# Four waits moved, and h and the layer weights as float16 halves, in a two-layer graph network kernel on one core

## The reference

```
h = relu(layernorm(x))
x = x + relu([h, segment_sum(h[src], dst), segment_sum(edge_attr, dst)] @ L0_W.T + L0_b)
h = relu(layernorm(x))
h1 = relu(segment_mean(h[src], dst) @ W1_l + b1 + h @ W1_r)
h2 = relu(segment_mean(h1[src], dst) @ W2_l + b2 + h1 @ W2_r)
x = x + h2
```

## Time and profile before

| what | value |
|---|---|
| median of 3 runs | 1438.12 us (1434.83 to 1440.58) |
| the profiled execution, its own time | 1440.59 us |
| its span, first to last instruction | 1438.8 us |
| mean granted TensorE clock | 0.984 |
| TensorE (PE) busy | 1356.1 us, 94% |
| VectorE (DVE) busy | 808.3 us, 56% |
| GpSimd (POOL) busy | 653.0 us, 45% |
| ScalarE (ACT) busy | 492.2 us, 34% |

### The profile page before, as it was taken

How to read it: one execution, slowest core, us unless ns; L and a number is a source line. 1 busy time by engine, 2 the same in 40 slices (tenths; PEclk the granted TensorE clock), 3 DMA queues, 4 the chain that set the end, 5 groups by cost and what they waited for, 6 DMA issues and landing times.

```text
span 1438.8 us, 34983 instructions
## 1 busy us (share of the span) xinstructions
PE 1356.1 (94%) x12154; PEld 1229.2 (85%) x12155; DVE 808.3 (56%) x1830; ACT 492.2 (34%) x1398; POOL 653.0 (45%) x771
## 2 busy tenths in 40 slices
PE   3768999999999999999999999999999999999995
PEld 3657999999999998998888888788888888888884
DVE  8678999898888888883444545422222223222221
ACT  2731123456788888882232232211111110000000
POOL 5400001111112212116777666377777645777775
PEclk9978999999999999999999999999999999999997
DMA  6109678888899898886564565565656666666662
GB/s 183 29 2 250 201 221 244 240 247 258 262 269 273 264 274 263 255 261 204 200 216 156 166 234 141 181 204 191 208 186 203 169 203 193 220 209 217 212 214 62
DMA packets 284723, 294.49 MB, mean 205 GB/s; under 512 B 19461, under 2 KB 250064, under 8 KB 284672
## 3 DMA queue, kind: packets, MB, share of 16 engines
q1 hardware_dynamic: 233861, 212.90, 46.9%
q0 software_dynamic: 26016, 69.24, 17.1%
q10 hardware_dynamic: 24795, 11.74, 2.8%
HBM read 245.70 MB, written 48.11 MB: 204 GB/s over the span
## 4 chain that ended last, share of the span: by engine, by line
PE 70%; POOL 15%; issue 7%; DMA 3%; ACT 3%; DVE 3%; SPq 0%; ACTq 0%; POOLq 0%; DVEq 0%
PE edge_banks L1126 27%; PE edge_banks L1064 20%; POOL shared L862 15%; PE banks L1038 10%; PE edge_banks L1060 4%; PE edge_banks L1103 3%; PE banks L1144 3%; DMA x_sb<-in_x 1%; PE banks L926 1%; ACT own L1274 1%; DMA shared<-g_rows,list_src 1%; ACT shared L1331 1%; PE edge_banks L1133 1%; DVE edge_t L1482 1%; PE banks L1138 1%
## 5 line engine op out<-in xcount | busy, mean ns | idle before, releaser
L862 POOL DMA_INDIRECT shared<-g_rows,list_src x555 | 540.1, 973 | 232.3 <-issue 168.7
L1126 PE MATMUL edge_banks<-g_even,shared 128*128 128x257 f16 (+1 forms) x3822 | 443.3, 272 | 1.2 <-DVE shared L1690 1.2
L1126 PEld LDWEIGHTS edge_banks<-g_even,shared 128*128 128x128 fp8e3 x3822 | 371.5, 97 | 58.9 <-DVEq L1659 1.4
L1064 PE MATMUL edge_banks<-shared 128*128 128x128 f32 x2744 | 344.5, 276 | 7.0 <-issue 6.6
L1064 PEld LDWEIGHTS edge_banks<-shared 128*128 128x128 f32 x2744 | 324.8, 192 | 10.5 <-issue 10.4
L841 POOL DMA_DIRECT2D counts<-shared x156 | 76.4, 490 | 484.5 <-ACT shared L1331 469.3
L1716 DVE SCALAR_TENSOR_TENSOR shared<-edge_banks,shared,own 128x128 f32<-128x128 f32 x98 | 34.4, 351 | 367.9 <-PE edge_banks L1126 339.2
L1126 PE MATMUL edge_banks<-shared 128*128 128x256 f16 x1911 | 225.7, 272 | 0.2 <-DVE own L1698 0.2
L1627 DVE TENSOR_TENSOR shared<-iota,shared 128x3528 f16<-128x3528 f16 x98 | 195.5, 1995 | 39.6 <-PE banks L1038 39.2
L1331 ACT ACTIVATE shared<-banks 128x392 uint16<-128x392 f32 x312 | 152.1, 488 | 179.2 <-PE banks L1038 169.3
L1126 PEld LDWEIGHTS edge_banks<-shared 128*128 128x128 fp8e3 x1911 | 185.2, 97 | 30.7 <-DVE own L1698 0.5
(11 more groups left out here) (282 smaller groups left out, 982.1 us busy)
## 6 DMA issues: line engine op xcount, KB each, us to landing
shared<-in_edge_attr SPq DMA_DIRECT2D x195, 512.0 KB, 4.5
shared<-counts SPq DMA_DIRECT2D x117, 784.0 KB
counts<-shared POOLq DMA_DIRECT2D x156, 196.0 KB, 4.0
shared<-g_rows,list_src POOLq DMA_INDIRECT x555
shared<-hot_rows SPq DMA_DIRECT2D x20, 304.0 KB
g_rows<-g_even SPq DMA_DIRECT2D x1, 3136.0 KB, 15.7
g_rows<-shared ACTq DMA_DIRECT2D x49, 64.0 KB
g_rows<-g_even ACTq DMA_DIRECT2D x49, 64.0 KB
```

The source lines that it names most:

```text
L862: pool.indirect_dma_start(ring_g[use % RING][:, t, 0:2 * D], None, g_rows[r], bass.IndirectOffsetOnAxis(ap=list_src[:, at:at + 1], axis=0) ...
L1064: mm = pe.matmul(edge_wide[bank][:, :, at], ring[:, bank * GROUP_TILES + j, :], hot_dst[u][:, k, (j - 1) * SPREAD:j * SPREAD].unsqueeze(1) ...
L1126: mm = pe.matmul(acc[s][:, 0:wide], stream8[slot][:, order[h], :], G[r % 2][:, order[h], 0:wide], start=h == 0, stop=h == BLOCKS - 1, skip ...
```

## The change

1. *First one-hots.* VectorE's wait for `zeroed` at the start of the build becomes a wait for `list_turned` (signalled after the last transposes of the lists, before the zeros); the wait for `zeroed` stands before the first `hot_dst` now.
2. *Places of the lists.* In rounds 0 and 1 the first eight lists stand at 5, 10, ..., 40. Round 2 is unchanged. The list of the last target block has 15 tiles in place of 18, in all rounds.
3. *Last list in two parts.* The last 5 gathers of round 2's last list signal a semaphore of their own, and TensorE waits for it only before the last 5 tiles.
4. *End behind the branch.* SyncE, ScalarE and VectorE load the verdict once it is there and take the branch before their last work (the last block on VectorE, its store on ScalarE, the wait for the stores on SyncE).
5. *Halves.* In rounds 0 and 1, h is written as two float16 halves. In round 0 three VectorE instructions do it in place of the one on ScalarE; in round 1 two in place of one. The turn is two float16 matmuls of 128 columns with an identity; ScalarE's copy then moves 256 columns, to float16. The layer weights are split into halves and scaled once (`split_weights`, ahead of round 0's first block on VectorE), and the dense product is three float16 matmuls of 256 columns. The own term's instruction (L1698) becomes one with a scale.

```diff
-LIST_AT = (tuple(range(6, LOOP_TO, TURN_OF)) + (44, 47),) * 2 + (tuple(range(6, LOOP_TO, TURN_OF)) + (45, 48),)
+LIST_AT = (tuple(range(5, LOOP_TO[0], TURN_OF)) + (44, 47),) * 2 + (tuple(range(6, LOOP_TO[2], TURN_OF)) + (45, 48),)
+LAST_BLOCK_TILES, LATE_TILES = 15, 5
...
+        def tiles_of(k):
+            return LAST_BLOCK_TILES if DENSE + list_of(k) == BLOCKS - 1 else LIST_TILES[k % 2]
+        def late_tiles(r, k):
+            return LATE_TILES if r == ROUNDS - 1 and k == LISTED - 1 else 0
...
-                                                    ).then_inc(list_landed[use % RING], 16)
+                                                    ).then_inc(late_landed if late else list_landed[use % RING], 16)
...
                         for t in range(tiles):
+                            if late_tiles(r, k) and t == tiles - late_tiles(r, k):
+                                pe.wait_ge(late_landed, 16 * late_tiles(r, k))
...
-                            pe.transpose(turn_ps[o], h_blk[:, o, :], ident[:, :]).then_inc(R["turned"], 1)
+                            for k in range(2):
+                                mm = pe.matmul(turn_ps[o][:, k * D:(k + 1) * D], h16[:, o, k * D:(k + 1) * D], turn16, start=True, stop=True)
+                            mm.then_inc(R["turned"], 1)
...
-                            pe.matmul(g_ps[o], hT_blk[:, o, :], w_conv[:, 2 * to - 2:2 * to, :].rearrange("p k f -> p (k f)"),
-                                      start=True, stop=True).then_inc(R["g_up"], 1)
+                            high, low = hT16[:, o, 0:D], hT16[:, o, D:2 * D]
+                            pe.matmul(g_ps[o], high, w_high[:, to - 1, :], start=True, stop=False, skip_group_check=True)
+                            pe.matmul(g_ps[o], low, w_high[:, to - 1, :], start=False, stop=False, skip_group_check=True)
+                            pe.matmul(g_ps[o], high, w_low[:, to - 1, :], start=False, stop=True, skip_group_check=True).then_inc(R["g_up"], 1)
...
                     if r == 0:
                         pe.wait_ge(S["zeroed"], 2 * BANKS + 2 * NDUO)
+                        pe.wait_ge(S["w_edge_ready"], 2)
...
-                            act.activation(hT_blk[:, o, :], turn_ps[o], ACT.Copy).then_inc(R["hT_done"], 1)
+                            act.activation(hT16[:, o, :], turn_ps[o], ACT.Copy).then_inc(R["hT_done"], 1)
...
-                            act.activation(h_blk[:, s, :], x_sb[:, bs, :].rearrange("p a f -> p (a f)"), ACT.Relu,
-                                           bias=tiny[:, s, 2:3], scale=tiny[:, s, 1:2]).then_inc(R["h_done"], 1)
...
-                dve.wait_ge(S["zeroed"], 2 * BANKS)
+                dve.wait_ge(S["list_turned"], 1)
...
                         if first and u == 0:
+                            dve.wait_ge(S["zeroed"], 2 * BANKS)
                             dve.wait_ge(S["edge_cleared"], 3)
...
+                    link(dve.tensor_scalar(h_raw, a_x, tiny[:, s, 1:2], tiny[:, s, 2:3], ALU.mult, ALU.add))
+                    dve.wait_ge(R["turned"], n + 1)
+                    link(dve.tensor_scalar(h16[:, s, 0:D], h_raw, 0.0, None, ALU.max))
+                    dve.scalar_tensor_tensor(out=h16[:, s, D:2 * D], in0=h_raw, scalar=0.0, in1=h16[:, s, 0:D], op0=ALU.max, op1=ALU.subtract
+                                             ).then_inc(R["h_done"], 1)
...
+            held = sp.snap(verdict[0], donate=True, min_val=0, max_val=1)
             with sp.If(held < 1):
...
+            with sp.Else():
+                finish()
```

264 lines of the change are left out of this document (161 added, 103 removed).

## The result

| | kernel before | changed kernel |
|---|---|---|
| median of the runs | 1438.12 us (1434.83 to 1441.71, 5 runs) | 1428.82 us (1426.64 to 1431.87, 5 runs) |
| profiled execution, its span | 1440.59, 1438.8 us | 1431.87, 1430.1 us |

The ratio of the two is 0.9935, with a 95% interval of 0.9911 to 0.9960: 9.3 us faster. That lies in the range of the prediction (1414 to 1431) and under the 1430.9 that it called faster, but the sum said 16.0. The profiled executions differ by 8.7. So 7.3 us of the forecast gain are missing, and the rest of this text is about where they went.

The account below looks back on a forecast made before the run. TensorE, busy 94% of the span, was taken as the bound, except GpSimd in round 2. The terms summed to -16.0 us, carried from the profiled execution to the median: 1438.1 to 1422.1 us, range 1414 to 1431.

Parts of the forecast that it names:

- First one-hots: Start of the build: VectorE no longer idles for the zeros, first `hot_dst` moves by at most 1.5; -1.2 us.
- Halves on TensorE: Rounds 0 and 1: dense product 0.43 to 0.33 us, turn unchanged at 0.11; 98 blocks, -10.0 us.
- Halves on VectorE: Round 0: h comes 0.34 us later, covered in usual blocks; early turns after 10 lists wait 0.33 each, +3.3 us.
- Round beginnings: Starts of rounds 1 and 2: nothing covers the longer h chain and copy; +0.6 and +0.4 us.
- Places of the lists: Rounds 0 and 1: waits at place 47 go, -4.5 us; round 1's list at place 5 waits, +4.7 us.
- End of round 2: Three gathers less, -3.75 us, and 5 matmuls instead of 19 after the last landing, -3.4; together -7.1 us.
- Behind the branch: End of the span: verdict load and branch leave the path after VectorE's last instruction; -1.5 us (0 to -2.5).
- the first (a dearer turn): Rival: a turn in two matmuls costs 0.22 us instead of 0.11, +10.7, so 1432.8 us; chance 0.07.
- the fourth: Rival: slower than before, if VectorE's three chained instructions make round 0's usual turns wait; chance 0.03.
- the fifth: Rival: no part shows, something the rows don't name, such as fetching a longer loop's code, takes it back; 1438 us, chance 0.03.
- the second: Rival: more than summed; place 5's rows undisturbed, VectorE's chain fits before early turns, turn costs 0.08; 1416 us, chance 0.13.
- The third: Rival: VectorE's chain and GpSimd hinder each other, gathers held, early turns wait 0.7 us; +6, so 1428 us; chance 0.11.

Follow-up runs that it names:

- the combination: Changed kernel with round 1's lists at old places, round 0's edge term ahead of the turn, early turn behind 17 sums, build register operations added: 1417.77 us, ratio 0.9862.
- The experiment gives 6.2 us in round 1: Changed kernel plus register operations in the build, with round 1's lists back at their old places (first at 6): 1424.25 us, ratio 0.9909 to the kernel before.

## Why the prediction was right, and where it was wrong

*First one-hots, -1.2 (0 to -1.5).* Right in its place. From the start of ScalarE's clearing of `edge_t` (109.64 in the earlier trace rows) to the first `hot_dst` it was 7.05 us; in the changed kernel's timeline it is 115.16 - 109.48 = 5.68, with a wait for ScalarE, as the step said:

```profile
109.48 5.54 ACT L1348 ACTIVATE edge_t<-zeros 128x6400 f32<-128x6400 f16 x1
```

```profile
115.16 0.69 DVE L1680 TENSOR_TENSOR shared<-iota,shared 128x512 f32<-128x512 f16 x1 [0.49 <-ACT edge_t L1348]
```

That is -1.4. In the whole time it can't be told: kernels that are equal up to round 0's first sum reach it between 651.9 and 656.2 us. So the -1.7 of the first stage is luck as much as anything.

*Halves on TensorE, -10.0.* The step's prices were right (dense 0.33, turn 0.11). **What failed is that only the changed instructions were priced.** The edge term behind the turn went from 0.22 to 0.28. The experiment that only changes the order takes it back, so the cost isn't the edge term's but the place behind two short float16 matmuls. Over the 38 turns of round 0 that have an edge term behind them it adds up to 2.1 us, and the turns themselves to 0.3 (two halves of 0.055 to 0.067 against 0.108).

*Halves on VectorE, +3.3.* **This term was mis-sized: it cost 5.0 us.** The chain is 1.20 us long and not 0.87, so nine of the ten early turns of round 0 came late, by 4.3 us in all from start to start; the largest, 0.72 at place 45, is over the 0.7 that I had named as a sign of being wrong. That the list of waits says 3.3 as well is chance: it counts from modelled ends and holds 0.34 us of round 1's beginning. And **the margin of 1.1 us for all usual blocks was read off one block**: in six of the nine second blocks after a list VectorE, which makes two blocks' splits there, has h only at the last moment, and the turn comes 0.10 to 0.13 us late, 0.7 in all. The edge order, which brings TensorE to that turn 0.22 us later, gave 3.4 us in round 0: 2.1 are the edge term, 0.7 these turns, and most of the rest early turns that waited less.

*Round beginnings, +0.6 and +0.4.* Round 1's stands at 0.5: its first sums are 2.83 us ahead of before, the last ones of that block 2.34. *Weights, 0:* VectorE's preparations took 4.0 us, all under TensorE's first 39 sums.

*Places of the lists, -4.5 and +4.7.* Both waits at place 47 went, the new one came with 4.9. How much of that is the places and how much the three gathers fewer in the list at place 44 is open: in round 1 the wait fell from 1.0 to 0.2 at the old places, and stood at 1.1 there in the combination; for round 0's 3.5 us no run separates the two. **The term that was mis-sized is the wait: it was booked at its idle time.** With the clock behind it it costs 7.1 us by the rows. The experiment gives 6.2 us in round 1 and 7.9 in the whole, and shows that nothing stood against it: round 1 had no wait at place 47 worth the move. In the prediction had shown this very clock behind 8.4 idle us, and I used it for the last list but not for place 5.

*End of round 2, -7.1.* From GpSimd's first issue of round 2 to its last it is 226.40 us and was 230.39, and its first comes 0.7 us closer to the round's start: -4.7 where -3.3 was booked for that stage. The 5 matmuls after the landing save 3.5 us of VectorE's end, as forecast.

*Behind the branch, -1.5.* The size is as forecast where VectorE and the store behind it are what the end waits for: 3.1 in place of 4.6 to 5.2. **The step that failed is that these two gains were added.** Both shorten the way from GpSimd's last issue to the end, 12.65 us, and it doesn't get shorter than 10.1, because GpSimd's own DRAIN comes 9.8 after that issue. Of -4.9, 2.5 came through. On top of the new end the list in two parts is worth 1.0 us (11.1 against 10.1), not 3.4; on top of the two parts the new end is worth 0.2 (10.3 against 10.1), not 1.5. The trace of the kernel before had the bound already: GpSimd's DRAIN ended at 1436.2, so no more than some 2.5 us could be gained behind its last issue. Why the DRAIN goes on for 7.3 us after the last rows have landed is open, and no edit tried to shorten it.

The balance of the missing 7.3 us, from the starts of TensorE's rows. Lost beyond the sum: 2.1 (edge term) + 1.7 (turns that wait, 5.0 and not 3.3) + 0.3 (the turn itself) + 0.5 (a wait for `counts` behind the list at place 40 of round 0, which the kernel before doesn't have) + 2.3 (the clock behind place 5) + 2.4 (the end) = 9.3. Gained beyond it: 1.4 in round 2, 0.5 in front, which is within what runs differ by there, and 0.2 at place 47 of round 0. That is 7.2.

Of the rivals, the first (a dearer turn), the fourth and the fifth are excluded by rows, and so is the second: the rows for place 5 came late, the early turns waited, and the turn cost 0.11. The third's 1428 is near the measured time, but not for its reasons: the gathers weren't held, and the early turns were mostly 0.4 to 0.6 us late and not 0.7. What exists of its mechanism is the reverse of it (below). That the median fell inside the range, where the sum was 7.3 us off, owes something to a wide range. Another sign of error that I had named came: the second block after most lists, a usual one in my steps, shows a wait.

Whether the halves are worth having in the end: alone they gain nothing that was measured. In the combination they should be, by some 8 us; this is an estimate, from round 0 before less its wait (274.88 - 3.5 - 0.35 = 271.0, against 267.2) and round 1 (259.0 - 0.35, against 254.4), and no run shows it.

## What to carry to other kernels

Price the neighbours of a replaced instruction too: an instruction that is made shorter can stop covering the weight load of the next one, and the order of two pieces was worth 1.2% of round 0 here. Book a long wait of TensorE with the slow matmuls behind it, and look for what the work behind the wait would have cost at full clock. When two savings lie on one way to the end, look for the third path that has been waiting beside them before adding them up; here the last instruction of each engine's queue, in the trace of the kernel before, would have shown it ahead of any run.

## What the runs showed of the hardware

*VectorE is held by GpSimd's gathers, not the reverse.* L1796 is a float32 to float16 relu. Of 48 in round 0, 18 began 0.52 to 0.68 us after a gather's start; they took 0.48 to 0.31, and all ended 0.99 to 1.00 after that start. The 30 others, begun earlier or behind the gather, took 0.23. L1794 was held the same way four times (begun 0.49 to 0.54 after the start, ended 0.99 after it), but not where it began 0.75 or later. One of either kind (timeline of the changed kernel):

```profile
752.88 0.94 POOL L893 DMA_INDIRECT shared<-g_rows,list_src  x1 [0.31 <-issue]
...
753.42 0.45 DVE L1796 TENSOR_SCALAR shared<-shared 128x128 f16<-128x128 f32 x1
```

```profile
746.64 0.95 POOL L893 DMA_INDIRECT shared<-g_rows,list_src  x1 [0.30 <-issue]
...
747.01 0.23 DVE L1796 TENSOR_SCALAR shared<-shared 128x128 f16<-128x128 f32 x1
```

L1797, with two operands in SBUF, took 0.29 all 48 times, 12 of them begun 0.48 to 0.78 after a gather's start, and the gathers' median is 0.945 (0.944 before). The Trainium skill (GPSIMD Engine Reference, Key points) names both kinds, instructions with two SBUF inputs and those in a two-port mode, as contending with GpSimd. Here the two that were held, L1796 and L1794, have one tensor input each, L1797 with two was not, and it was VectorE that waited. In which mode they ran no run shows.

*The clock after idle stretches.* In the kernel before, a wait of 3.53 us left the clock at 2.4 GHz. With the edge term first, one of 3.53 (round 1, place 5) was followed by 1.2 GHz (0.50 from 958 to 960), and in the kernel of the halves alone even one of 3.23 (round 2, place 45; 0.50 from 1406 to 1408). Waits of 3.58 (before the last 5 matmuls), 3.66, 4.88, 5.19 and 8.42 us ended at 1.2 GHz, those up to 1.1 us at 2.4. So around 3.5 us the length of a wait didn't decide it here. The Trainium skill (TensorE: Matmul & The Clock Gate, Part 1) has the same two levels, the lower one for an engine that was idle; the rows agree, with the 3.53 us of the kernel before as the exception.

*GpSimd's end.* In each of eight profiles (the changed kernel, and its variants beside 1438 us except the halves alone) GpSimd's DRAIN ended 9.8 us after the start of its last gather, 7.3 after the rows had landed; in the kernel before and in the halves alone it was 10.1 to 10.2.

*A chip on which TensorE's own stream stalls.* On one chip every kernel, the one before too, took 2000 to 2024 us; the four profiles from it have "issue" ahead of some 280 matmuls in the rounds, in one stretch of each pass of the loop. In the other runs no kernel had more than 0.4 us of it in the rounds. What the stream waited for is not in the trace and stays open.
